# Seven rank pieces of graph one and the normalising of its rows, computed in the removal stage, with one buffer shared by all stages

## The reference

```
def step(carry, n):                      # node after node, n = 0..1023
    row = jnp.take(carry, n, axis=0)
    nbi = row.astype(jnp.int32)
    num = jnp.sum(nbi)
    sf = jnp.where(num > T_DIL, (num + K_DIL - 1) // K_DIL, 1)
    rank = jnp.cumsum(nbi)
    rm = row & (rank % sf == 0)
    valid = (mask_b[n] != 0) & (num > 1)
    rm = jnp.where(valid, rm, False)
    keep = ~rm
    carry = carry.at[n].set(row & keep)
    carry = carry.at[:, n].set(carry[:, n] & keep)
    return (carry, None)
...
keep = jax.vmap(_dilate_pattern)(adj > 0, mask)
return adj * keep.astype(adj.dtype)
```

## Time and profile before

| | us |
|---|---|
| three timed runs | 1236.42, 1240.63, 1240.42 |
| their median | 1240.42 |
| the profiled execution | 1238.54 |
| its span | 1236.8 |

### The profile page before, as it was taken

How to read it: one execution, slowest core, us unless ns; L and a number is a source line. 1 busy time by engine, 2 the same in 40 slices (tenths; PEclk the granted TensorE clock), 3 DMA queues, 4 the chain that set the end, 5 groups by cost and what they waited for, 6 DMA issues and landing times. The chain is left out here.

```text
span 1236.8 us, 26874 instructions
## 1 busy us (share of the span) xinstructions
PE 1134.6 (92%) x9697; PEld 928.9 (75%) x9713; DVE 769.1 (62%) x2811; ACT 602.9 (49%) x1557; POOL 114.6 (9%) x129
## 2 busy tenths in 40 slices
PE   3999899987599999999899999999998899996998
PEld 3999766664388889888699998799998455543554
DVE  5999588777457777765435354345454655646973
ACT  3888567677646666663223334223334523314341
POOL 3333000000000000000000000123131111100000
PEclk9999888886799999999899999999999999998999
DMA  8977112110356666664157571166673355634911
GB/s 327 334 275 281 48 25 35 29 28 15 138 196 254 260 253 267 261 258 164 51 194 303 193 302 49 51 243 269 227 300 138 137 203 212 266 136 186 397 47 51
DMA packets 105514, 228.93 MB, mean 185 GB/s; under 512 B 34528, under 2 KB 53152, under 8 KB 105376
## 3 DMA queue, kind: packets, MB, share of 16 engines
q1 hardware_dynamic: 104656, 227.07, 49.5%
q10 hardware_dynamic: 720, 0.07, 0.1%
HBM read 185.70 MB, written 37.75 MB: 181 GB/s over the span
## 5 line engine op out<-in xcount | busy, mean ns | idle before, releaser
L1485 PE MATMUL lay_acc<-lay_z,k_otheradj 128*128 128x128 f32 x1024 | 118.4, 277 | 0.0
L1485 PEld LDWEIGHTS lay_acc<-lay_z,k_otheradj 128*128 128x128 f32 x1024 | 117.2, 194 | 0.0
L1485 PE MATMUL lay_acc<-lay_z,k_keepadj 128*128 128x128 f32 x1024 | 117.0, 275 | 0.0
L1485 PEld LDWEIGHTS lay_acc<-lay_z,k_keepadj 128*128 128x128 f32 x1024 | 115.6, 192 | 0.0
L1533 ACT ACTIVATE lay_junk<-lay_o 128x128 bf16<-128x128 f32 x128 | 37.7, 295 | 124.6 <-DVEq L1622 124.4
L1599 DVE TENSOR_TENSOR lay_o<-lay_ring,k_vec 128x512 f32<-128x512 f32 x32 | 22.1, 692 | 108.8 <-PE lay_ring L1478 108.8
L1579 POOL TENSOR_TENSOR lay_bl<-k_vec,k_mask 128x256 f32<-128x256 f32 x32 | 21.2, 662 | 572.4 <-DVEq L1612 568.7
L333 PE MATMUL att_acc<-att_rhs,att_adjT 128*128 128x130 f32 x512 | 59.7, 280 | 14.0 <-POOLq L285 12.3
L333 PEld LDWEIGHTS att_acc<-att_rhs,att_adjT 128*128 128x128 f32 x512 | 59.0, 195 | 14.6 <-POOLq L285 12.4
L1541 ACT ACTIVATE lay_o<-lay_o,lay_nrm 128x128 f32<-128x128 f32 x128 | 39.3, 388 | 53.5 <-DVE lay_nrm L1633 53.5
L1192 ACT ACTIVATE fuse_dist<-fuse_prank,k_kb 128x512 f16<-128x512 f32 (+2 forms) x64 | 38.8, 606 | 51.9 <-PE fuse_prank L1082 49.5
(11 more groups left out here) (294 smaller groups left out, 2537.8 us busy)
## 6 DMA issues: line engine op xcount, KB each, us to landing
k_keepadj<-in_adj_cols SPq DMA_DIRECT2D x28, 1024.0 KB, 8.9
k_keepadj<-keptT SPq DMA_DIRECT2D x12, 2048.0 KB, 11.0
k_otheradj<-keptT SPq DMA_DIRECT2D x12, 2048.0 KB, 10.9
att_adjT<-in_adj_cols SPq DMA_DIRECT2D x16, 1024.0 KB, 8.1
k_otheradj<-in_adj_cols SPq DMA_DIRECT2D x16, 1024.0 KB, 10.6
keptT<-k_keepadj SPq DMA_DIRECT2D x16, 1024.0 KB, 4.6
keptT<-k_otheradj SPq DMA_DIRECT2D x16, 1024.0 KB, 4.7
lay_rowf<-in_adj_rows SPq DMA_DIRECT2D x32, 512.0 KB, 14.6
```

The source lines that it names most:

```text
L1485: mm = t.matmul(acc[i % 2][k][:, ib % HB, :], adjT[i % 2][:, jb, ib * P:(ib + 1) * P], zz[i % 2][:, jb, :], start=(jb == 0), stop=(jb == N ...
```

## The change

In removal, three functions are added. At the end of each block from the second on, PE sums the ranks of one row block of graph one over its first up to 512 columns (`near_ranks`), between the counts of two groups of graphs; it takes a slot of the PSUM ring for it. ACT turns it into a distance in one of two new buffers (`near_distances`), after the last `current` of the block and before the next distances. DVE compares a block later, in the first round (`near_removals`), the last of the seven at the end of the stage. The normalising of graph one's rows moves on ACT from the end of the stage to the end of its first block.

In the keep stage the 12 pieces of graph one become 5 (`left`): columns 512 and up of blocks 4 to 7, and the first 512 columns of block 7. The other graphs keep 12.

The `low` buffer is now resident for the whole program, and the other stages put their by-products into it: `prod`, `sink` and three constant tiles of attention, two of the three row buffers and `bl` of the layers, `spare` and `rcol` of the last two blocks. No DMA is added, removed or moved in its queue.

```
+        near_dist = [s.sb(f"near_dist{i}", [P, HALF], F16) for i in range(2)]
+        near_ready, near_read = s.sem("near_ready"), s.sem("near_read")
...
+                def near_ranks(nb):
+
+                    o = take()
+                    top = min(HALF, (nb + 1) * P)
+                    for jb in range(min(nb, HALF // P - 1) + 1):
+                        mm = t.matmul(o[:, jb * P:top], T8[:, 0, jb, nb * P:(nb + 1) * P], K["fore8"][:, 0:top - jb * P],
+                                      start=(jb == 0), stop=(jb == min(nb, HALF // P - 1)))
+                    mm.then_inc(ring_ready, 1)
...
                         if nb > 0:
                             current(prev, third)
                             far_counts(prev, second)
+                            near_ranks(prev)
...
+                def near_distances(nb):
+
+                    if nb >= 2:
+                        act.wait_ge(near_read, nb - 1)
+                    o = take()
+                    top = min(HALF, (nb + 1) * P)
+                    a.activation(near_dist[nb % 2][:, 0:top], o[:, 0:top], ACT.Abs, bias=K["kb"][:, nb:nb + 1])
+                    act.drain().then_inc(near_ready, 1)
+                    act.sem_inc(ring_free, 1)
...
                     if nb > 0:
                         current(prev, second)
                         current(prev, third)
+                        near_distances(prev)
+                    else:
+                        norm_apply(nc, act, lambda t: K["X"][:, t, :], K["h"][:], row, 0, first_h)
                     if more:
                         distances(nb, first)
-                norm_apply(nc, act, lambda t: K["X"][:, t, :], K["h"][:], row, 0, first_h)
                 distances(NB - 1, range(B))
...
+                def near_removals(nb):
+
+                    dve.wait_ge(near_ready, nb + 1)
+                    top, c0 = min(HALF, (nb + 1) * P), low_columns(nb)
+                    v.tensor_scalar(K["low"][:, c0:c0 + top], near_dist[nb % 2][:, 0:top], K["kd"][:, nb:nb + 1], None, ALU.is_equal)\
+                        .then_inc(near_read, 1)
...
                         if nb > 0 and k < 3:
                             staying(prev, (first, second, third)[k])
+                        if nb > 1 and k == 0:
+                            near_removals(nb - 2)
...
                 v.tensor_tensor(K["kbhigh"][:], high, lowcount[:], ALU.add)
+                near_removals(NB - 2)
                 staying(NB - 1, range(B))
...
+    early = [q for q in range(NP) if pieces[q][0] < NB - 1 and pieces[q][1] == 0]
+    left = [q for q in range(NP) if q not in early]
...
-        low = s.sb("low", [P, low0[NB]], BF16)
+        low = K["low"]
...
-        def of_block(nb):
-            return [q for q in range(NP) if pieces[q][0] == nb]
+        def of_block(b, nb):
+            return [q for q in (left if b == 0 else range(NP)) if pieces[q][0] == nb]
+
+        def piece_number(b, q):
+            return left.index(q) if b == 0 else b * NP + q - len(early)
...
-                        pe.wait_ge(low_ready, (b + 1) * NP)
+                        pe.wait_ge(low_ready, (b + 1) * NP - len(early))
...
-        prod = s.sb("prod", [P, 2, NB, D], BF16)
+        prod = K["low"][:, 0:2 * N].rearrange("p (k t d) -> p k t d", k=2, d=D)
...
-            resident("spare", [P, 2 * N])
+            K["spare"] = K["low"][:].bitcast(F32)
```

More of the change, by code:

```diff
@@ L184, in attention_phase @@
         rhs = [s.sb(f"rhs{i}", [P, NB, PITCH], F32) for i in range(2)]
-        prod = s.sb("prod", [P, 2, NB, D], BF16)
+        prod = K["low"][:, 0:2 * N].rearrange("p (k t d) -> p k t d", k=2, d=D)
         w = norm_buffers(s.sb, s.sem, "n", NB)
-        sink = s.sb("sink", [P, N], BF16)
+        sink = K["low"][:, 2 * N:3 * N]
         minus_half = s.sb("minus_half", [P, NB], F32)
@@ L201, in attention_phase @@
         maskf = maski[:].bitcast(F32)
-        dstep = s.sb("dstep", [P, P], BF16)
-        dfore = s.sb("dfore", [P, P], BF16)
-        dlow = s.sb("dlow", [P, P], BF16)
+        dstep, dfore, dlow = (K["low"][:, 3 * N + i * P:3 * N + (i + 1) * P] for i in range(3))
         pset = s.ps("pset", [P, HALF])
@@ L485, in _, with low_columns @@
                 v.tensor_scalar(K["maskok"][:], K["mask"][:], 0.0, None, ALU.not_equal)
+def low_columns(nb):
+    return P * nb * (nb + 1) // 2
 def removal_phase(nc, z, A, K):
@@ L981, in fuse_phase @@
               if hf * HALF < (nb + 1) * P]
-    low0 = [sum((i + 1) * P for i in range(j)) for j in range(NB + 1)]
+    low0 = [low_columns(j) for j in range(NB)]
     NR, NM = 2, 2
@@ L1072, in ranks @@
                 def ranks(b, nb):
-                    for q in of_block(nb):
+                    for q in of_block(b, nb):
                         _, lo, hi = pieces[q]
-                        n = b * NP + q
+                        n = piece_number(b, q)
                         if n >= NR:
@@ L1266, in removals @@
                 def removals(b, nb):
-                    for q in of_block(nb):
+                    for q in of_block(b, nb):
                         _, lo, hi = pieces[q]
-                        n, tile = b * NP + q, b * NB + nb
+                        n, tile = piece_number(b, q), b * NB + nb
                         dve.wait_ge(dist_ready, n + 1)
@@ L1403, in layer_phase @@
     with Scope(nc, f"lay{layer}") as s:
-        bl = s.sb("bl", [P, 2, D], F32) if final else None
+        bl = K["low"][:].bitcast(F32)[:, 2 * N:2 * N + 2 * D].rearrange("p (t d) -> p t d", d=D)
         x_added = s.sem("x_added")
@@ L1411, in layer_phase @@
         w = dict(col=s.sb("col", [P, 8], F32), var_ready=s.sem("var_ready"), dev_ready=s.sem("dev_ready"))
-        rowf = [s.sb(f"rowf{i}", [P, N], F32) for i in range(NF if PER else 0)]
+        rowf = [K["low"][:].bitcast(F32)[:, i * N:(i + 1) * N] for i in range(2)] + [s.sb("rowf2", [P, N], F32)[:]]
         row_loaded = [s.sem(f"row_loaded{i}") for i in range(NF)]
@@ L1440, in load_row @@
                         sp.wait_ge(row_bits, q - NF + 1)
-                    sp.dma_start(rowf[q % NF][:], block_rows(A["adj_rows"], g, jb)).then_inc(row_loaded[q % NF], 16)
+                    sp.dma_start(rowf[q % NF], block_rows(A["adj_rows"], g, jb)).then_inc(row_loaded[q % NF], 16)
                 for q in range(NF if PER else 0):
@@ L1578, in _ @@
                         x = K["X"][:, tile:tile + 2, :]
-                        g.tensor_tensor(bl[:], along_tiles(K["vec"][:, V_BL, :], 2), along_features(K["mask"][:, tile:tile + 2], D),
+                        g.tensor_tensor(bl, along_tiles(K["vec"][:, V_BL, :], 2), along_features(K["mask"][:, tile:tile + 2], D),
                                         ALU.mult)
                         pool.drain()
-                        g.tensor_tensor(x, x, bl[:], ALU.add)
+                        g.tensor_tensor(x, x, bl, ALU.add)
                         pool.drain()
@@ L1641, in row_compare @@
                     dve.wait_ge(row_loaded[q % NF], 16 * (q // NF + 1))
-                    v.tensor_scalar(row_slot(T8, g, jb), rowf[q % NF][:], 0.0, None, ALU.is_gt, saturate=False).then_inc(row_bits, 1)
+                    v.tensor_scalar(row_slot(T8, g, jb), rowf[q % NF], 0.0, None, ALU.is_gt, saturate=False).then_inc(row_bits, 1)
                 def beside(i):
@@ L1949, in maxdeg_phase @@
         res = [s.sb(f"res{i}", [P, NB, D], F32) for i in range(2)]
-        rcol = s.sb("rcol", [P, z.T], F32)
+        rcol = K["spare"][:, 2 * N:2 * N + z.T]
         w = norm_buffers(s.sb, s.sem, "n", NB)
@@ L2080, in finish @@
                     v.scalar_tensor_tensor(r, r, 0.0, K["X"][:, cols, :], ALU.max, ALU.add).then_inc(res_ready, 2 * (hi - lo) // NB)
-                v.reciprocal(rcol[:], K["colsum"][:])
+                v.reciprocal(rcol, K["colsum"][:])
                 mean(1)
@@ L2131, in build_program @@
         resident("h", [P, z.NB, D])
+        resident("low", [P, low_columns(z.NB)], BF16)
         with ExitStack() as codes:
```

## The result

| | before | after |
|---|---|---|
| runs compared | 13 | 13 |
| median (us) | 1236.63 | 1235.45 |
| lowest to highest | 1235.44 to 1240.63 | 1233.52 to 1236.17 |
| ratio, 95% interval | | 0.9976 [0.9965, 0.9987] |
| profiled execution, its span | 1238.54, 1236.8 | 1236.12, 1234.3 |

By the ratio the change gains 3.0 us (0.0024 x 1236.6; interval 1.6 to 4.3). The medians are only 1.2 us apart. Neither figure is sharp, because before's times fall in groups: eight at 1235.4 to 1236.9, two at 1238.6 to 1238.7, three at 1240.2 to 1240.6. After's 13 times all lie at 1233.5 to 1236.2. Against the lowest group alone (median 1236.3) after is 0.9 us faster. The profiled execution of before (1238.54) is one of the middle group.

A forecast was written before the change was run, and what follows sets the result against it. Keep stage bound by PE, removal by a chain between PE, DVE and ACT with none full. Normalising -2.3, head -2.9, removal costs +1.2 give -4.0: from 1239.5 to 1235.5 us, range 1231 to 1240.

The forecast's parts named there:

- Normalising: End of removal: eight distances start at 314.28 instead of 316.61, gain 2.33; its new place in block 0 costs 0.
- can PE deliver that piece in time: End of removal: PE's last early piece is done at 313.3, just fits; if late by 1.05, gain 1.3.
- Head: Keep stage's head: seven pieces leave, first mask 11.0 us after start against 13.9; gain 2.9, range 2.2 to 3.8.
- no load of the head is waited for, a gain here stays: Keep stage: PE bounds the rest and no load is waited for, so the head's 2.9 stays.
- Rival 2: Keep stage: clock rises after the masks begin, 2.9 us more at half clock; 1238.4, no change; chance 0.12.
- masks at a clock of 0.5: Keep stage: granted clock of 0.5 at the masks, listed as a sign that the prediction is wrong.
- Costs in removal: Inserted pieces in removal: PE 0.6, ACT 0.1, DVE 0.5, sum 1.2; bounds 0.3 and 8.0 to 10.1.
- Rival 3: Ends of removal's blocks 1 to 6: inserted work lies on the chain, +2.8 to +4.9, 1242.3 to 1244.4; chance 0.07.
- Sum and base: Whole kernel: -2.3 - 2.9 + 1.2 = -4.0, from 1239.5, the middle between profile 1238.54 and median 1240.42, to 1235.5.
- Rivals 1 and 4: 1: removal costs hidden, head gives 3.8, clock earlier; 1232.8, chance 0.24. 4: first mask waits for something else; 1238.4, chance 0.02.

The follow-up runs named there:

- experiment 1: Changed kernel with only the shared buffer left: twelve pieces of graph one in the keep stage, normalising back at the end of removal; ratio to before 0.9999.
- 2: experiment 1 with the normalising early, still no early pieces; ratio to before 0.9967.
- experiment 5: Changed kernel plus 14 unused matmuls on PE after removal's last block, before the keep stage; ratio to before 0.9945, median 1230.32.
- 10: Changed kernel plus 8 unused matmuls in PE's waits within the keep stage's head; ratio to before 0.9943.
- experiment 11: Changed kernel plus unused matmuls in the head and 14 at removal's end, paced by DVE's last instructions; ratio to before 0.9928, median 1229.59.
- 4: Changed kernel with all twelve pieces computed again in the keep stage, the early ones in removal kept as extra work; ratio to before 0.9976.
- 3: Changed kernel with the normalising back at the end of removal: shared buffer and early pieces alone; ratio to before 1.0001.
- experiment 9: Changed kernel with the pieces' ranks later in removal's blocks, behind the last counts and DVE's release; ratio to before 1.0004, median 1238.96.
- 7: Changed kernel plus 12 unused matmuls on PE behind its last piece of removal, before it reads the flag; ratio to before 0.9956.
- 6: experiment 1 plus 26 unused matmuls on PE at the end of removal; ratio to before 0.9996.
- experiment 8: Shared buffer and early normalising without early pieces, plus 13 unused matmuls before removal's last flag; ratio to before 0.9954.
- 12: Early normalising without early pieces, plus the unused matmuls of experiment 11 at both places; ratio to before 0.9959, median 1233.84.

## Why the prediction was right, and where not

**Normalising.** Right in mechanism: the distances start 1.30 after the last `current` ends (forecast 1.02), and its new place costs nothing (block 0 is 10.42 long before and after). The end gave 1.77 instead of 2.06 (2.33 less DVE's 0.27). The question "can PE deliver that piece in time" was answered with "just"; it was late by 0.20 (ACT waited 0.38, not 0.18), and the step from the piece to the first distance is 0.24, not 0.15. Experiments 1 and 2 put the normalising alone at 3.11, and the pieces take 1.33 of it back (19.60 against 18.27), where 0.85 and DVE's 0.27 were reckoned.

**Head.** Right: 2.86 for 2.9. The projection started 3.65 after the stage's start (forecast 3.7) and the first mask at 11.06 (forecast 11.0). One price in it was misread: the projection of 1.78 was taken as half clock, but the clock rose at about 327.6, within it; wholly at half clock it took 2.07.

**The step that failed: "no load of the head is waited for, a gain here stays".** It did not stay. Rival 2, given 0.12, happened: the masks began at 0.50, and 2.32 of the 2.86 went back (2.9 was its price). The profile of before had the sign of it: the head was at half clock until about 327.6, and the clock rose while the work was running that the change takes out. I argued from the projection of 1.78 in one piece; after, it took 2.07 at 0.50 and the clock stayed there. The condition that I wrote as a sign of error ("masks at a clock of 0.5") is met. Experiments 5, 10 and 11 show the mechanism by taking it away; 4 shows it by putting the pieces back. It is no matter of one profile: with five pieces and no unused matmuls (after, 3, 9) the head is at 0.50 and the first mask takes 0.61, with twelve (before, 1, 2, 4) it takes 0.39. Only the price varies: masks to `k_Wx` took 5.37, 5.52 and 4.58, which is 1.5 to 2.5 over 3.05. The Trainium skill ("TensorE: Matmul & The Clock Gate", section "What's actually happening") says that the low clock is the default and that activity releases it: the runs agree (0.50 with PE busy for 7.66 of 11.08 us, 0.66 and full clock at the masks with 9.02 of 10.60).

**Costs in removal.** Forecast 0.9 for blocks 1 to 6, with 0.3 to 10 as bounds. Against before it is 0.73; against experiment 1 it is 1.65 (block 3 +0.57, 4 +0.27, 5 +0.42, 6 +0.22). No pair settles the size: blocks 0 to 6 took 143.56 to 144.92 in the seven kernels with the pieces at this place (after, 3, 4, 5, 7, 10, 11) and 143.12 to 145.10 in the six without (before, 1, 2, 6, 8, 12). What the rows do show is DVE's wait for PE at the starts of blocks 4 and 5: 2.19 and 2.73 in after, 1.87 and 2.48 in experiment 1 (below), 0.57 more together. That is PE's part at the ends of blocks 3 and 4; the forecast had the first at 0.33 and the second as hidden. Where the rest lies is open. Rival 3 did not happen, but experiment 9 shows that one other placement brings much of it: its removal is 5.5 longer than after's.

```profile
241.39 0.17 DVE L957 TENSOR_TENSOR rem_w<-rem_pl,rem_w 128x8 f32<-128x8 f32 x1 [1.87 <-PEq L746]
...
261.23 0.17 DVE L957 TENSOR_TENSOR rem_w<-rem_pl,rem_w 128x8 f32<-128x8 f32 x1 [2.48 <-PEq L746]
```

**Sum and base.** -4.0 was forecast, -2.50 stands between the spans, -3.0 [-4.3, -1.6] by the ratio, -1.2 between the medians. The +2.32 was missed; -0.95 came from ahead of removal's first block, where no instruction was changed and where experiment 1 has it too (155.19). That part is chance. So is the hit of 1235.5 on 1235.45: the base of 1239.5 was 2.9 above before's median, and the gain of 4.0 was 2.8 above the distance of the medians, so the two errors cancel. The base itself depends on how many runs fall in which group: in three further series before's median was 1238.2 to 1238.4.

**Rivals 1 and 4** did not happen: the clock came later, not earlier, and the first mask waited for its last compare, as it should.

What stays open: why before's times form groups. A possible reason is in the last section; it was not tested.

## What to carry to other kernels

Before taking work out of the head of a stage, look at the granted clock there: where it is at half, that work may be what raises it, and the time saved can be paid back by the first dense work behind. Price the removed work with the clock that the remaining work will have. Where an engine idles into a barrier and the next stage begins with short bursts, a few unused matmuls up to the barrier and between the bursts gave more here (ratio 0.9928 against 0.9976, 5.9 us) than the reordering did (3.0 us by its ratio); where they ended 3.6 us early most of it was lost (1.1 of 4.6 us was left), and if they are late they hold the barrier up.

## What was unexpected

**A gain far behind the change.** The unused matmuls of experiments 5, 10 and 11 gain 2.5 to 2.9 us more in the span than up to `k_Wx` (experiment 11: 6.7 and 3.85); the rest comes later in the program. Stretches of after, then of experiment 11, about the start of the layers (the counterpart of 589 in after is about 585 there) and in them:

```profile
589.00:595.00 6.00, 2.08 (x10) 1.14 (x8) 1.73 (x6) 4.29 (x16) 0.00 (x0) 0.73 0.00 0
595.00:601.00 6.00, 4.79 (x12) 1.74 (x13) 2.37 (x7) 0.29 (x1) 0.00 (x0) 0.50 0.62 220
601.00:607.00 6.00, 6.00 (x51) 5.91 (x50) 2.10 (x5) 1.19 (x2) 0.00 (x0) 0.92 0.12 45
770.00:810.00 40.00, 36.77 (x282) 31.29 (x281) 14.86 (x36) 6.64 (x20) 6.15 (x8) 0.96 0.20 70
```

```profile
585.00:591.00 6.00, 2.23 (x11) 1.13 (x8) 1.70 (x7) 4.46 (x17) 0.00 (x0) 0.78 0.00 0
591.00:597.00 6.00, 4.62 (x19) 2.27 (x20) 2.55 (x7) 0.29 (x1) 0.00 (x0) 0.65 0.58 199
597.00:601.70 4.70, 4.70 (x45) 4.70 (x44) 2.09 (x5) 1.19 (x2) 0.00 (x0) 1.00 0.21 85
770.00:810.00 40.00, 36.98 (x313) 34.46 (x312) 17.85 (x41) 7.07 (x28) 11.05 (x15) 1.00 0.37 139
```

The step from the last sum of the keep stage to the first of the layers takes 23.9 us in after and 22.3 to 22.6 in experiments 5, 10 and 11; from there to the last sum of the two layers it is 348.5 and 347.2. The code there is the same: the layers open, in before as well, with twelve unused matmuls, which took 5.28 in before, after and experiment 1, and 4.13, 4.36 and 4.11 in experiments 5, 10 and 11. So how long PE stays at 0.50 at the head of a stage differs between kernels whose code there is the same. When the stage begins does not decide it alone: the layers begin at 591.82 in experiment 5 and at 592.02 in experiment 8, where the twelve took 5.28 and the two lengths are 23.9 and 348.5, as in after. PE of experiment 5, then of experiment 8:

```profile
591.82 4.13 PE L1410 MATMUL lay_acc<-k_fore,k_ident 128*128 128x512 fp8e5 x12 [2.24 <-PEq L140]
```

```profile
592.02 5.28 PE L1405 MATMUL lay_acc<-k_fore,k_ident 128*128 128x512 fp8e5 x12 [2.24 <-PEq L140]
```

Such differences may also be what puts the times of unchanged code at 1236, 1238.5 or 1241 us: argued, not shown.
